# Relation sums of a graph layer: one-hot rows of the tally made by GpSimd, tile by tile, instead of by VectorE for eight tiles at once

## The reference, cut to what matters

```python
# _L0_gnn_ref, 200000 edges, sorted by dst, 8 relations
hx = jnp.einsum('ni,rio->rno', x, weight)
msg = hx[edge_type, src]                                  # one row of 256 per edge
agg = jax.ops.segment_sum(msg, dst, num_segments=num_nodes)
```

```python
# _L0_ffn_ref, over edge_index of 131072 edges
denom = jax.ops.segment_sum(ee, dst, num_segments=M)
agg = jax.ops.segment_sum(msg, dst, num_segments=M)
```

## Time and profile before

| what | value |
|---|---|
| median of 3 runs | 4519.31 us |
| lowest and highest of the 3 | 4509.97 and 4532.03 us |
| span of the profiled execution | 5377.8 us |
| of that, the stage relation_sums | 897 to 2451 us |
| GpSimd busy in it | 1001.5 us, 1040 gathers |

### The profile page before, as it was taken

How to read it: one execution, slowest core, us unless ns; L and a number is a source line. 1 busy time by engine, 2 the same in 40 slices (tenths; PEclk the granted TensorE clock), 3 DMA queues, 4 the chain that set the end, 5 groups by cost and what they waited for, 6 DMA issues and landing times. The chain is left out here.

```text
span 5377.8 us, 72916 instructions
## 1 busy us (share of the span) xinstructions
PE 3810.4 (71%) x19358; PEld 2805.1 (52%) x19383; DVE 2664.5 (50%) x9403; ACT 1681.8 (31%) x4007; POOL 2947.9 (55%) x2997
## 2 busy tenths in 40 slices
PE   4888886854555555546687777787766788887798
PEld 2455553743333333335565666665525666776566
DVE  7655532543435333325332333333795666666782
ACT  3334443222223222223233333333542222222330
POOL 5777765566666666661554455544165555555121
PEclk9999998977667677765888888888888999999798
DMA  6444444343333333332321222221638888998001
GB/s 220 157 155 149 158 158 145 90 130 88 88 90 88 91 91 90 93 94 30 80 46 41 47 46 47 44 49 37 218 125 287 291 297 301 313 311 286 14 1 48
DMA packets 351400, 690.67 MB, mean 128 GB/s; under 512 B 70225, under 2 KB 173918, under 8 KB 344635
## 3 DMA queue, kind: packets, MB, share of 16 engines
q0 software_dynamic: 139328, 355.39, 22.9%
q1 hardware_dynamic: 211677, 330.60, 18.8%
HBM read 573.39 MB, written 112.35 MB: 128 GB/s over the span
## 5 line engine op out<-in xcount | busy, mean ns | idle before, releaser
L1007 POOL DMA_INDIRECT e_ring<-table,erow x1040 | 1001.5, 963 | 539.2 <-issue 272.4
L1349 PE MATMUL e_sums<-e_ring,e_onehot 128*128 128x257 f32 x2080 | 765.4, 508 | 611.3 <-DVE e_onehot L1262 298.4
L2445 POOL DMA_INDIRECT t_source<-source_rows,t_index x632 | 598.2, 947 | 595.6 <-DVE t_parts L2531 394.8
L1349 PEld LDWEIGHTS e_sums<-e_ring,e_onehot 128*128 128x128 f32 x2080 | 412.5, 238 | 783.4 <-issue 378.3
L1461 POOL DMA_INDIRECT e_ring<-table,esrc x544 | 531.4, 977 | 391.2 <-PE e_sums L1558 239.9
L554 POOL DMA_INDIRECT r_ring<-rows,esrc x528 | 585.8, 1110 | 246.6 <-issue 131.7
L985 ACT ACTIVATE k_sign<-ramp,low 128x128 bf16<-128x128 f32 x1024 | 349.8, 393 | 968.6 <-DMA r_xw<-rows 443.1
L1546 PE MATMUL e_total<-e_loads,e_times 128*128 128x256 f32 x3072 | 519.6, 306 | 1.2 <-issue 1.2
L2640 PE MATMUL t_out<-t_w,t_hidden 128*128 128x256 f32 x1600 | 438.8, 410 | 100.9 <-issue 98.1
L1222 DVE SCALAR_TENSOR_TENSOR big<-e_sums,within,big 128x257 f32 x130 | 62.9, 484 | 826.9 <-remote 666.6
L1444 ACT ACTIVATE e_times<-e_tally 128x320 fp32r<-128x320 f32 (+4 forms) x640 | 255.6, 426 | 668.8 <-PE e_tally L1530 288.8
(11 more groups left out here) (532 smaller groups left out, 6372.0 us busy)
## 6 DMA issues: line engine op xcount, KB each, us to landing
e_loads<-table SPq DMA_DIRECT2D x512, 256.0 KB
table<-r_stage SPq DMA_DIRECT2D x49, 1024.0 KB
outputs<-first_outputs SPq DMA_DIRECT2D x49, 512.0 KB, 6.8
first_outputs<-t_stage SPq DMA_DIRECT2D x96, 256.0 KB
t_near<-near_rows SPq DMA_DIRECT2D x79, 256.0 KB
e_ring<-table,erow POOLq DMA_INDIRECT x1040
table<-n_split SPq DMA_DIRECT2D x49, 256.0 KB
t_source<-source_rows,t_index POOLq DMA_INDIRECT x632
```

The lines of the kernel that those rows point to most:

```text
L1007: eng.indirect_dma_start(ring[:, t % RING, 0:D], None, table, bass.IndirectOffsetOnAxis(ap=b.erow[:, EARLY + t:EARLY + t + 1], axis=0)).th ...
L1349: eng.matmul(sums[g % SUMS][:, 0:ACCW], onehot[t % ONEHOTS][:, :], ring[:, t % RING, :], start=(t % GROUP == 0), stop=(t % GROUP == GROUP ...
L2445: eng.indirect_dma_start(source[s][:, q, :], None, a.source_rows, bass.IndirectOffsetOnAxis(ap=index[s][:, q:q + 1], axis=0)).then_inc(gat ...
```

## The change

GpSimd now makes the one-hot rows of the tally: one tile's, 128x49, ahead of each of the first 1024 gathers. Its `mark(t)` waits until the tally of tile t - 24 has been multiplied, whose place in `hot` it takes, then compares. VectorE's `mark` of 128x392 is gone, with its 128 instructions. The tally on TensorE waits for its own tile's rows (`highed` at t + 1) where it waited for its group's.

```diff
         @block.gpsimd
...
+            def mark(t):
+                wait_if(eng, tallied, t - HIGHS * GROUP + 1)
+                eng.tensor_scalar(hot[t // GROUP % HIGHS][:, t % GROUP, :], b.ramp[:, 0:NW], b.high[:, t:t + 1], None,
+                                  ALU.is_equal).then_inc(highed, 1)
+
             for t in range(TILES):
+                if t < GT:
+                    mark(t)
                 if t >= RING:
                     eng.wait_ge(summed, t - RING + 1)
                     eng.sem_inc(cleared, 1)
...
-            def mark(u):
-
-                wait_if(eng, tallied, GROUP * (u - HIGHS + 1))
-                eng.tensor_tensor(hot[u % HIGHS][:, :, :], b.ramp[:, 0:NW].unsqueeze(1).broadcast_to([P, GROUP, NW]),
-                                  b.high[:, GROUP * u:GROUP * (u + 1)].unsqueeze(2).broadcast_to([P, GROUP, NW]),
-                                  ALU.is_equal).then_inc(highed, 1)
-
...
-            mark(0)
             for t in range(TILES):
...
-                if t % GROUP == 2 and t // GROUP + 1 < TALLIED:
-                    mark(t // GROUP + 1)
...
             def tally(t):
                 eng.wait_ge(signed, t + 1)
-                eng.wait_ge(highed, t // GROUP + 1)
+                eng.wait_ge(highed, t + 1)
```

## The result

The changed kernel takes 4950.8 us (median of 4 runs, 4949.7 to 4956.4) against 4519.1 us: a ratio of 1.0956, 95% interval 1.094 to 1.0972, **9.6% slower**. The direction and the mechanism of the prediction held; its 4759 us and the top of its range, 4900 us, did not. The loss is 432 us where 240 were forecast.

A forecast was written before the change was run, and what follows sets the result against it. The prediction took GpSimd's queue of gathers, 1.25 us a tile, to bound the stage. Comparisons 256, plus contention 14, less 30 hidden, made 240 us: 4519 + 240 = 4759 us, range 4560 to 4900.

The forecast's parts named there:

- The bound: In the changed stage, GpSimd's queue of gathers sets the time: 1040 x 1.25 = 1300 us.
- the surplus of 858 us: Profiled span 5377.8 against median 4519.3 us; claimed to be waits in the profiled execution alone, about 248 us in this stage.
- main case: Without the profile the stage runs at GpSimd's cadence, so comparisons add time: 4650 to 4870 us, chance 0.55.
- rival A: Ring waits are in every run, so GpSimd's 227 us of slack hide most comparisons: 4560 to 4640 us, chance 0.20.
- The price of a comparison: On GpSimd, each 128x49 comparison between two gathers takes 0.25 us: 1024 x 0.25 = 256 us.
- The estimate of 0.07 us a comparison: GpSimd's comparison priced from the Trainium skill's cycle rate: 72 us in all, about 4590 us; set aside for the trace's row.
- The lower row: GpSimd's two-tensor instruction as the comparison's price from below: 0.17 us each, 174 us in all.
- Contention: GpSimd comparisons held up by VectorE's one-hots, one in seven meeting one: 14 us taken, 205 us kept for the range.
- Rival D: Every GpSimd comparison meets a VectorE one-hot and is held up: 431 us, 4950 us; chance 0.11, shared with a dearer comparison.
- Hidden: Comparisons cost nothing where GpSimd would wait for the ring: 30 us taken for the early 104 tiles, between 0 and 227.
- Removed: VectorE's 128 `mark` instructions, 61 us, come off its wait for TensorE: 0 on the path, at best -61 us.
- The added waits: GpSimd's wait for the tally 24 tiles back and TensorE's wait for its own tile's rows: cost 0.

The follow-up runs named there:

- before_fourth: The kernel before, no edit, traced again on fast chip 0: 4528.8 us, its stage 1341 us.
- the earlier trace: The kernel before, no edit, profiled ahead of the prediction: span 5377.8 us, that of a slow chip, its stage 1554 us.
- no_rows_3: The kernel before without VectorE's row making, GpSimd only filling `hot` three times at the start; on a fast chip 4510.7 against 4521.6 us.
- the removal alone: The kernel before with nobody making the tally's rows, constants multiplied instead: ratio 1.0016 on a slow chip, 0.9975 on a fast one.

## Why the prediction was right or wrong

**The bound.** Right, but the step that led there was wrong and came out by luck. GpSimd's cadence of 1.25 us sets the stage, and there are no ring waits where the time was measured (before_fourth). The reason given was that the surplus of 858 us is in the profiled execution alone; a slow chip has it without a profile too. The choice between the main case and rival A was in truth the choice between two kinds of chip. Rival A's mechanism, 227 us hidden, is what the slow chips do: 433 us of comparisons cost 219 there (1024 x 0.423; 433 - 227 = 206 by A's sum), 215 us cost 2 to 8, 174 us cost nothing. The stage of the earlier trace rows was forecast to grow to between 1600 and 1720 us on such a chip; it took 1772, again by the price of a comparison.

**The price of a comparison.** Here the step failed: "The slope is 1.17 / 256 = 4.6 ns a column, and 49 columns come to 0.03 + 0.22 = 0.25 us". It took its fixed part from a one-column MEMSET, another operation, and put the rest on the columns. Ahead of a gather the same operation costs 0.28 us at one column, not 0.03, and a further column 2.4 to 2.9 ns, not 4.6. Both ends of the range for this term, 0.17 and 0.25, lay below the measured 0.42, and this term is nearly all of the miss: 1024 x (0.42 - 0.25) = 174 of the 192 us. A line through one width of one operation and one width of another is no bound from above; the 1.20 us of the same operation at 256 columns would have been one. So the column's price was too high and the fixed part far too low. The estimate of 0.07 us a comparison, 72 us in all, was further off still.

**The lower row.** The two-tensor add was priced at 0.17 and measured at 0.17, alone and in the whole kernel (+177 us). It adds two tensors and does not compare with a scalar, so it is not the change's work.

**Contention.** 14 us were taken, and about 12 came. Take the usual distance of two gathers (the median, 1.251 us alone and 1.674 with a comparison between) off every step: 29 us of lengthened steps are left after, and 17 in the kernel in which nobody makes the rows (no_rows_3). The changed kernel's comparisons last 442 ns in the median and 477 in the mean:

```profile
L1005 POOL TENSOR_SCALAR k_hot<-ramp,high 128x49 bf16<-128x49 f32 x1024 | 488.8, 477 | 34.9
```

Rival D, all of them held by one-hots, would have given 4950 us and so the very time that was measured, by another cause. It is ruled out. It needs comparisons of uneven length, and the distance between gathers is 1.66 us at the tenth part and 1.76 at nine tenths. More directly, VectorE is idle for long stretches, as here from 1606.11 to 1617.42:

```profile
1604.39 1.72 DVE L1261 TENSOR_SCALAR e_onehot<-ramp,edst 128x128 f32<-128x128 f32 x8
1617.42 0.48 DVE L1229 SCALAR_TENSOR_TENSOR big<-e_sums,within,big 128x257 f32 x1 [11.31 <-PE e_sums L1346]
```

In 568 of the 1039 steps from gather to gather no VectorE instruction runs at all, and their median is 1.674 us too. Long comparisons as in the earlier trace rows occur, but they are exceptions: 7 of 1024 last over 1 us, the longest 2.35, and five of these stand beside VectorE's addition of the bias (`features<-features,e_bias`), a 2.0 us instruction of two inputs.

**Hidden.** 30 us were taken for the early tiles, and no ring waits were there. That is another 30 us of the miss.

**Removed.** 0 taken, with a few microseconds from less contention mentioned; 11 us measured on the fast chip and 12 in its trace, nothing on the slow one. It is the contention, as said under the removal alone, and not the 61 us of VectorE's time. The added waits cost nothing that shows: TensorE's waits are for landings and for one-hots, none for the tally's rows.

With what the traces show the prediction's own sum reads 433 for the price (1024 x 0.423), 12 for contention, 0 hidden and 12 given back: 433 us. From first to last gather the traces differ by 1761.3 - 1329.1 = 432 us, and the times by 432.

## What to carry to other kernels

Price an instruction on GpSimd by the distance between its neighbours' starts, and from the same operation at two widths; a fixed part that is borrowed from a fill was wrong by nine times here (0.03 against 0.28 us). A GpSimd that issues gathers back to back had no room for the comparison, whatever its busy share says: it was busy 1014 us of 1341, 76%, and full. Work for an engine that shows waits is free only if those waits exist on the chip that will run it, so look at a trace from the chip that gave the time.

## What the runs showed of the hardware

The same program takes 4522 us on chip 0 and 5389, 5342 and 5336 us on chips 7, 15 and 8, while GpSimd's cadence is the same, 1.251 to 1.254 us in the median. This stage has 210 to 224 us of the surplus; the rest lies in other stages, since the changed kernel takes the same time in this stage on both kinds of chip and still 611 us more in all. What lies behind it was not found, but the trace of before shows where in this stage it enters. It is not the length of TensorE's multiplies: `add` starts late after them.

```profile
1592.51 1.11 PE L1349 MATMUL e_sums<-e_ring,e_onehot 128*128 128x257 f32 x4
1606.14 0.48 DVE L1222 SCALAR_TENSOR_TENSOR big<-e_sums,within,big 128x257 f32 x1 [13.13 <-remote]
```

The second of these four multiply passes, which ended at 1593.19, was the last of the group that this `add` takes, so `add` started 12.95 us behind it. In the median over the groups that distance is 4.5 us in this trace, at most 27.8, against 0.15 us in before_fourth. "Remote" is a release for which the trace has no instruction of this core; it ended 656 of 812 us of VectorE's idle time ahead of `add`, and before_fourth has none there (653.7 of 654.9 us were ended by the multiply itself). So the prediction's reading, that VectorE waits there for TensorE, holds on the fast chip and is open on the slow one. GpSimd's waits for a ring slot, up to 5.4 us, are ended by "remote" as well in 156 us of the earlier trace rows.

A gather's reported span changes with its neighbour: 0.95 us behind a gather, 1.03 behind a comparison and 0.96 behind the two-tensor add, with the pause ahead of it at 0.30, 0.16 and 0.16. Only the distances add up.
